# Two more destination windows of a relational layer made into blocks

## What is computed

```
norm = deg_inv_sqrt[row] * deg_inv_sqrt[col] * edge_weight
xw   = einsum('ni,tio->tno', x, W)                 # 4 types
out  = segment_sum(xw[edge_type, col] * norm[:, None], row) + b
x    = leaky_relu(out, 0.01)
```

## Time and profile before

| | |
|---|---|
| median of three runs | 8893.29 us |
| profiled execution | 8904.66 us, its span 8902.9 us |
| busy in the span | PE 4999.8, DVE 3817.0, POOL 3452.0, ACT 790.4 us |
| GAT edge pass with blocks | 3410 to 4746 us |
| relational layer's rounds | 5519 to 7147 us |
| last edge pass, no blocks | 7269 to 8606 us |

### The profile page before, as it was taken

How to read it: one execution, slowest core, us unless ns; L and a number is a source line. 1 busy time by engine, 2 the same in 40 slices (tenths; PEclk the granted TensorE clock), 3 DMA queues, 4 the chain that set the end, 5 groups by cost and what they waited for, 6 DMA issues and landing times. The chain is left out here.

```text
span 8902.9 us, 107716 instructions
## 1 busy us (share of the span) xinstructions
PE 4999.8 (56%) x20390; PEld 2829.2 (32%) x21197; DVE 3817.0 (43%) x7633; ACT 790.4 (9%) x2438; POOL 3452.0 (39%) x3466
## 2 busy tenths in 40 slices
PE   7771111888887764666763365767776633333331
PEld 6640000444443332333332253444444411111120
DVE  6760001666668824333336475111121143333346
ACT  1100000000000000111111101000000001111110
POOL 0287776000000004565551200664646625555531
PEclk6695555999998886777775598778787765555555
DMA  4200000001115554555552254445464422222210
GB/s 119 74 1 9 2 2 1 22 22 37 37 37 189 216 186 111 149 151 159 150 150 57 68 145 148 162 158 188 157 200 161 148 76 60 60 59 59 61 41 23
DMA packets 516087, 857.86 MB, mean 96 GB/s; under 512 B 97507, under 2 KB 363896, under 8 KB 480772
## 3 DMA queue, kind: packets, MB, share of 16 engines
q1 hardware_dynamic: 405534, 680.93, 23.6%
q0 software_dynamic: 110432, 175.35, 8.7%
HBM read 647.06 MB, written 208.91 MB: 96 GB/s over the span
## 5 line engine op out<-in xcount | busy, mean ns | idle before, releaser
L915 PE MATMUL psum<-hot_src,hot_dst 128*128 x4836 | 1156.0, 376 | 933.7 <-DVE hot_dst L850 628.0
L2291 POOL DMA_INDIRECT l_gathered<-l_table,l_st x960 | 916.2, 954 | 1118.2 <-issue 906.3
L848 DVE TENSOR_SCALAR hot_src<-count_iota,tile_shifted 128x3200 f16 x806 | 850.8, 1056 | 1025.1 <-remote 688.3
L1609 POOL DMA_INDIRECT l_edges_by_src<-l_by_src,l_edges_st x816 | 796.4, 976 | 990.9 <-ACT l_edges_st L1639 458.0
L412 POOL DMA_INDIRECT by_src<-src_rec,src_pos x784 | 879.5, 1122 | 572.5 <-ACT attr_turned L714 333.9
L1609 POOL DMA_INDIRECT l_edges_by_src<-l_q,l_edges_st x816 | 772.6, 947 | 722.7 <-ACT l_edges_st L1652 319.4
L915 PEld LDWEIGHTS psum<-hot_src,hot_dst 128*128 x5642 | 565.7, 101 | 1523.0 <-issue 1100.7
L1674 PE MATMUL psum<-l_k_parts,l_edges_hot_t 128*128 x2448 | 461.9, 289 | 940.6 <-issue 775.6
L2319 DVE TENSOR_SCALAR l_hot<-iota,l_loc,l_weight 128x128 f32<-128x128 f32 x960 | 261.8, 356 | 1228.0 <-remote 976.6
L1513 PE MATMUL psum<-pair_hot_weight,pair_hot_dst 128*128 128x512 f32 x1100 | 701.6, 777 | 134.1 <-issue 72.9
L2360 PE MATMUL psum<-l_blocks,l_rows 128*128 128x512 f32 (+1 forms) x1680 | 724.8, 591 | 11.1 <-issue 8.1
(11 more groups left out here) (431 smaller groups left out, 5382.5 us busy)
## 6 DMA issues: line engine op xcount, KB each, us to landing
l_blocks<-pair_blocks SPq DMA_DIRECT2D x180, 1024.0 KB
l_sum_counts<-counts SPq DMA_DIRECT2D x75, 1600.0 KB, 7.5
pair_blocks<-pair_block SPq DMA_DIRECT2D x25, 2560.0 KB
l_edges_loc<-loc_by_tile SPq DMA_DIRECT2D x416, 128.0 KB
l_rows<-l_edges_by_src SPq DMA_DIRECT2D x204, 256.0 KB
l_sum_rows<-l_rows SPq DMA_DIRECT2D x204, 256.0 KB
counts<-attr_then_counts SPq DMA_DIRECT2D x25, 1600.0 KB
attr_then_counts<-in_edge_attr SPq DMA_DIRECT2D x14, 1568.0 KB
```

Source lines behind the costliest of these rows:

```text
L848: v.tensor_scalar(hot_src[:, bass.ds(place, 1), 0:NP].rearrange("p a c -> p (a c)"), iota[:, :], shifted[:, 0, bass.ds(t, 1)], None, ALU.i ...
L915: ins = pe.matmul(k.ps[c][:, 0:m], hot_dst[:, bass.ds(place, 1), :].rearrange("p a c -> p (a c)"), hot_src[:, bass.ds(place, 1), col:col + ...
L1609: pool.indirect_dma_start(a[:, r, g, :], None, table_src, bass.IndirectOffsetOnAxis(ap=st[:, r, g:g + 1], axis=0))\
L2291: pool.indirect_dma_start(sent[:, p, g, :], None, by_type, bass.IndirectOffsetOnAxis(ap=st[:, p, g:g + 1], axis=0))\
```

## The change

Two more entries of 1 in `CAPS`, so that destination windows 10 and 11 (nodes 1280 to 1535) get one tile of block edges a source window; and the ring of PSUM banks in `PairBlocks` follows KD.

```
-CAPS = (7, 3, 2, 2, 2, 2, 1, 1, 1, 1)
+CAPS = (7, 3, 2, 2, 2, 2, 1, 1, 1, 1, 1, 1)
 KD = len(CAPS)
 S = sum(CAPS)
 HT = -(-W * S // CH) * CH
...
-    STEPS, PARTS, RING, PLACES = 2, 2 * R, 5, 4
+    STEPS, PARTS, RING, PLACES = 2, 2 * R, KD // 2, 4
```

## The result

The changed kernel takes 9342.14 us (median of four runs, 9337.81 to 9353.55) against 8893.35: ratio 1.0506, 95% interval 1.0487 to 1.0524. It is 449 us slower. The forecast was 9400 us, slower. The profiled execution went from 8904.66 to 9337.81 us, its span from 8902.9 to 9335.8, +433 us; the working is compared with that.

The account below looks back on a forecast made before the run. The relational rounds were taken as bound by the loop of gathers, PE and staging, no engine full. Rounds +457, last shares +9, block pass +40, rest +2 made +508 us on 8893.3: 9401, rounded to 9400 us; range 9320 to 9500.

Parts of the forecast that it names:

- The number of shares: Relational rounds: SHARES as a floor makes 24 shares a round in place of 20, 384 gathers, 118 tiles padding.
- Periods with real gathers, 382 us: Relational round: 16 periods between shares at 24.0 us, less 2 us for the short one, 382 us.
- Padding, 1.3 us a gather and 31 us a period: Late in a relational round: padding gathers hold all DMA engines 1.3 us each; 7.4 periods of 31 us, 220 us.
- The rivals at 24 and 41 us a period: Late periods: padding hides like real gathers (24 us, 9237 us, 15%) or jams the loop (41 us, 9610 us, 15%).
- The last share, +3 us: End of each relational round: the last share, now all padding, takes 3 us more, +9 us in all.
- The block pass, +40 us: Attention pass that makes the blocks: extra pairs and evacuations partly covered, +40 us, bounds 0 and +100.
- The rival of a PE-bound pass: Block-making pass becomes PE-bound: +100 to +140 us in place of +40, 9460 to 9500 us; 8%.
- The rest, +2 us: Longer list and edge buffer, and two short DVE steps more: +2 us; all other passes the same.
- The sum: Whole kernel: 457 + 9 + 40 + 2 = +508 us.
- Faster if the share count followed the tiles: Relational rounds: with 17 groups run, 84 us saved less 42 elsewhere, 8851 us; rival, 4%.

Follow-up runs that it names:

- Version 2: Kernel before with SHARES = 24 in place of 20 and nothing else, on chip B: 7602.4 us, ratio 1.049.
- version 1: Changed kernel with SHARES = 17 in place of 24, all else equal, on chip B: 7137.1 us, ratio 0.985.
- experiment 9: Kernel before with dummy matmuls beside 4, then 11, of the 22 pairs of a source window, chip A: block pass 1353.3 and 1347.7 us.

## Why the prediction was right, point by point

- *The number of shares.* Right: 24 a round, 1152 gathers. Version 2 shows that the constant alone slows the kernel, version 1 that removing the floor turns the sign.
- *Periods with real gathers, 382 us.* 378.7, 374.1 and 377.4 us, so 16 us too much in three rounds. A period is 23.5 us in the mean, no longer than before, so the third dense step cost nothing of the 0.3 us that I gave it.
- *Padding, 1.3 us a gather and 31 us a period.* 1.29 us, and 211.6, 211.0 and 212.4 us for seven periods, 30.2 each, against 220: 25 us too much. The engines were 95 to 98% busy where I had taken 90%, so the period is near the sum of its DMA work, 28.6 us. The rivals at 24 and 41 us a period are refuted by these rows.
- *The last share, +3 us.* It took 19.2 us in the mean of the rounds, before 18.2.
- *The block pass, +40 us.* This is the term that was mis-sized: about 0 in the pair that the sum is held against (+0.5 us) and on chip B (-0.1), +15.2 in the second pair on chip A, where repeats of one kernel differ by 5 and 10 us. I had read PE, DVE and ACT as links of the chain because ACT's staging follows DVE's consume. The links have slack: in the first pair POOL waits 291.1 us for ACT's staging (L1652) in this pass before and 291.9 after, and on the faster chip 14.6 us without the new pairs (version 2) and 11.6 with them (version 1). There the pass stands at 1042 us, 5.1 us a group, which is POOL's issue of four gathers and hardly more, and experiment 9 adds PE work without stretching it much. The rival of a PE-bound pass falls with it. What makes POOL wait those 291 us on chip A is open.
- *The rest, +2 us.* From the block pass's last gather to the first dense matmul the two pairs show 5.5 and 4.8 us more; the pass itself began 6.8 us earlier in one pair and 4.0 later in the other, so +2 is not told apart. The last pass, whose code is the same, took 1347.3 us against 1336.6 and, in the second pair, 1335.2 against 1331.5: what differs there by 4 to 11 us belongs to no edit.
- *The sum.* 508 forecast, 433 in the profiled pair. The rounds, from the first dense matmul to the last, took 421 us more where 466 were forecast; the last pass 11 more where none were; all the rest 1 us more where 42 were: 508 - 45 + 11 - 41 = 433. The second pair of traces gives 458 us, 429 of them in the rounds.
- *Faster if the share count followed the tiles.* Predicted as a rival: 84 us saved in the rounds, 42 given back elsewhere, so 42 us less. On chip B it is 114 us less, 0.985. Of those 42 us, 40 were the block pass that did not grow there.

## What to carry to other kernels

When a change moves work from one path to another, look up the code that turns the amount into a loop count: a floor, a rounding or a count tied to the same constant can raise the work that was to shrink. Let padding read where real data lie, spread over rows; weight zero makes its value harmless, not its transfer. A gathered loop with a ring has a price per turn, so count turns before engine time.

## What the runs showed of the hardware that I had not expected

Gathers of 64 KB from a table in HBM held the sixteen DMA engines 0.22 us (chip B; real ones 0.24 on chip A) when their 128 rows were spread, 0.49 us (chip C) when all 128 were one row that changed from tile to tile, and 1.29 us (A) and 1.32 us (B) when gather after gather read row 0.

One program took 8895 us on one chip and 7251 us on two others. On chip A long waits of DVE and ACT are put down to "remote", on chip B there are none. The counting loop's first instruction, in the kernel before on A, and in version 1 on B:

```profile
L848 DVE TENSOR_SCALAR hot_src<-count_iota,tile_shifted 128x3200 f16 x806 | 850.8, 1056 | 1025.1 <-remote 688.3 <-PE psum L915 231.1 <-issue 100.0
```

```profile
L848 DVE TENSOR_SCALAR hot_src<-count_iota,tile_shifted 128x3200 f16 x806 | 856.6, 1063 | 279.6 <-PE psum L915 238.0 <-issue 35.1
```

The instruction itself takes as long on both. What the waits are is open; each ratio is taken within one chip, and whether the change's 1.05 would be the same on chip B is not shown.
